# Global attention in arrays of its own, one layer's weight halves on chip, and new begin times, in an adaLN block with windowed attention

## The reference

```python
mod = (silu(c) @ wmod).reshape(8, 6, 1, 256)          # sa, ca, ga, sb, cb, gb
h = layernorm(x) * (1 + ca) + sa
x = x + ga * global_attention(h)                      # causal over 1024 rows, RoPE, one softmax per row
h = layernorm(x) * (1 + cb) + sb
x = x + gb * ffn(h)                                   # DEPTH = 2 local layers
# a local layer:
h = shift_token(x); q, k, v = split(h @ wqkv)         # 256 -> 3 x 512, 8 heads of 64
q, k = rotary_xpos(l2norm(q) * qs, l2norm(k) * ks)
x = x + local_attention(q, k, v) @ wo                 # windows of 128, each looks one window back
h = layernorm(shift_token(x)) * lg + lb
a, g = split(h @ w1 + b1); x = x + (a * gelu(g)) @ w2 + b2
```

## Time and profile before

| | |
|---|---|
| median of 3 runs | 2667.91 us (2666.67 to 2672.59) |
| the profiled execution's own time | 2665.09 us |
| its span, first to last instruction | 2663.3 us |
| TensorE matmul busy | 2533.0 us, 95% |
| VectorE, ScalarE, GpSimd busy | 85%, 73%, 49% |
| mean granted TensorE clock | 0.985 of full |
| DMA, mean over the span | 17 GB/s |

### The profile page before, as it was taken

The page is one execution under the profiler, slowest core; times in us unless marked ns, Lnnn a source line. Parts: engine busy times, 40 slices in busy tenths (PEclk is TensorE's granted clock), DMA queues, the critical chain, the costliest instruction groups (busy, mean ns, idle before and its releaser), DMA issues. The chain is left out here.

```text
span 2663.3 us, 71937 instructions
## 1 busy us (share of the span) xinstructions
PE 2533.0 (95%) x25566; PEld 1726.5 (65%) x25566; DVE 2274.1 (85%) x6823; ACT 1932.2 (73%) x4782; POOL 1300.6 (49%) x953
## 2 busy tenths in 40 slices
PE   7899989999899998999989999999999999989997
PEld 4566666667566665676656666666766666666675
DVE  8897889878898788987889878898889978799785
ACT  3598856878468784778747787587874888648884
POOL 2364534655355553555435554365544555445552
PEclk7999999999999999999999999999999999999999
DMA  5000010000100000000000000000000000000000
GB/s 190 21 7 8 5 43 2 9 6 8 39 3 9 6 16 30 4 10 4 18 29 5 9 5 20 25 6 8 6 19 25 6 8 6 19 25 6 7 6 21
DMA packets 51026, 46.49 MB, mean 17 GB/s; under 512 B 11530, under 2 KB 47980, under 8 KB 50548
## 3 DMA queue, kind: packets, MB, share of 16 engines
q1 hardware_dynamic: 50004, 40.78, 5.0%
q10 hardware_dynamic: 672, 1.10, 0.1%
HBM read 25.06 MB, written 8.42 MB: 13 GB/s over the span
## 5 line engine op out<-in xcount | busy, mean ns | idle before, releaser
L780 ACT ACTIVATE ar_b<-ar_b,small 128x192 f32<-128x192 f32 (+1 forms) x1024 | 445.3, 437 | 80.7 <-DVE small L1073 79.8
L1343 POOL TENSOR_TENSOR ar_c<-ar_c 128x1024 f32<-128x1024 f32 x128 | 302.7, 2365 | 284.0 <-DVE ar_c L1059 283.2
L1339 POOL TENSOR_TENSOR small<-small,neg_half 128x16 f32<-128x16 f32 x128 | 380.6, 2974 | 115.0 <-DVE small L1031 112.0
L1073 DVE CUSTOM_DVE_ANT_0 ar_b<-ps,mask_t,small 128x192 f32<-128x192 f32 x896 | 318.9, 411 | 27.0 <-PE ps L529 26.8
L1358 POOL TENSOR_TENSOR mlp<-mlp 128x512 f16<-128x512 f32 x160 | 198.0, 1243 | 204.2 <-ACT mlp L835 203.6
L160 PE MATMUL ps<-wqkv_hi,ht_hi 128*128 128x512 f16 x768 | 292.9, 381 | 0.0
L162 PE MATMUL ps<-wqkv_hi,ht_lo 128*128 128x512 f16 x768 | 291.6, 380 | 0.0
L161 PE MATMUL ps<-wqkv_lo,ht_hi 128*128 128x512 f16 x768 | 291.6, 380 | 0.0
L160 PE MATMUL ps<-ht_hi,w_hi 128*128 128x512 f16 (+1 forms) x704 | 269.1, 382 | 11.3 <-DVE ht_lo L1021 11.3
L162 PE MATMUL ps<-ht_hi,w_lo 128*128 128x512 f16 (+1 forms) x704 | 268.3, 381 | 0.0
L161 PE MATMUL ps<-ht_lo,w_hi 128*128 128x512 f16 (+1 forms) x704 | 268.1, 381 | 0.0
(11 more groups left out here) (197 smaller groups left out, 6911.7 us busy)
## 6 DMA issues: line engine op xcount, KB each, us to landing
xu<-in_L_attn_x_dram SPq DMA_DIRECT2D x32, 256.0 KB, 2.9
out_dram<-xu SPq DMA_DIRECT2D x64, 128.0 KB, 2.5
rows<-xu SPq DMA_DIRECT2D x128, 63.5 KB
mlp<-in_L_ffn_wqkv_dram SPq DMA_DIRECT2D x2, 1536.0 KB, 6.6
modb<-mod_rows SPq DMA_DIRECT2D x8, 384.0 KB, 4.3
rows<-in_L_ffn_w_dram SPq DMA_DIRECT2D x2, 1364.0 KB, 10.3
rows<-xu SPq DMA_DIRECT2D x112, 0.5 KB
ar_b<-in_L_wmod_dram SPq DMA_DIRECT2D x2, 768.0 KB, 7.1
```

The lines of the kernel that those rows point to most:

```text
L780: last = act.activation(pw, pw, ACT.Exp, bias=mnw[:, n % 2, h:h + 1], scale=-1.0, accum_out=smw[:, n % 2, h:h + 1])
L1073: last = dve.tensor_tensor_reduce(out=PW[:, pw_at(f, q, i) + c:pw_at(f, q, i) + KW], in0=ps[:, bk, i * KW + c:(i + 1) * KW], in1=mask, sca ...
L1339: pool.tensor_tensor(rinv[:, n % 4, :], ssm[:, n % 2, :], neg_half[:, 0:16], ALU.pow).then_inc(s_rinv, 1)
L1343: pool.tensor_tensor(M1[:, n % 2, :], M1[:, n % 2, :], M2, ALU.add).then_inc(s_add, 1)
```

## The change

- Global attention gets arrays of its own: a new `ar_g` (`xn1`, `hf1`, `ra`, `rb`, `P1`, `PT1` and new halves of h, `hg`), and the windows' `V`, `QT`, `KT` go into a new `ar_w`. Its waits for the last window of the batch before are gone. To fit, `xn1`, `hf1`, `rb`, `P1`, `PT1` hold one tile in place of two, and the windows' `V` three in place of four; so `rw`, `af`, `rp`, `pe` and `ph` now wait for the reader of the tile just before.
- The input rows are loaded into an array of their own, `XI`, almost a batch ahead.
- Only one layer's weight halves and xpos table stay on chip. The halves of both layers are stored in DRAM in the first batch (`tq`, `tw`, `tv`, `to`, `tx`), and each of the 15 further layers reloads its own: `lq` 1.5 MB, `lw` 1.4 MB, `lv` 0.79 MB, `lo` 0.52 MB, `lx` 1 MB, all issued by the sync engine on its one queue, in a place set by the table.
- `PERIOD` goes from 316.98 to 313.02, and all begin times are new.

```diff
-        wqkv_p = [sb(f"wqkv_{s}", [P, DEPTH, NC, 3 * INNER], F16) for s in ("hi", "lo")]
+        wq_r = sb("wqkv", [P, 2 * NC * 3 * INNER], F16)
+        wqkv_p = wq_r[:, :].rearrange("p (s c n) -> p s c n", s=2, c=NC)
...
+        XI = sb("x_in", [P, NT, DIM])
-        V = ar_a[:, 0:2048].rearrange("p (r n) -> p r n", r=4)
+        ar_w = sb("ar_w", [P, 16 * 256])
+        V = ar_w[:, 0:1536].rearrange("p (r n) -> p r n", r=3)
...
-        xn1 = ar_c[:, 0:1024].rearrange("p (r t c n) -> p r t c n", r=2, t=2, c=NC)
+        ar_g = sb("ar_g", [P, 20 * 256])
+        xn1 = ar_g[:, 0:512].rearrange("p (t c n) -> p t c n", t=2, c=NC)
+        P1 = ar_g[:, 2560:3584]
+        PT1 = [ar_g[:, 3584 + 512 * i:4096 + 512 * i].bitcast(F16).rearrange("p (k n) -> p k n", k=NT) for i in range(2)]
+        hg = [ar_g[:, 4608 + 256 * i:4864 + 256 * i].bitcast(F16).rearrange("p (c n) -> p c n", c=NC) for i in range(2)]
...
                         if b:
-                            sp.wait_ge(s_fin, (b - 1) * NT + 2 * p + 2)
-                        sp.dma_start(X[:, 2 * p:2 * p + 2, :],
+                            sp.wait_ge(s_x2, at("ys", b - 1, 2 * p + 1))
+                        sp.dma_start(XI[:, 2 * p:2 * p + 2, :],
...
+                    elif k == "lq":
+                        L = piece[1]
+                        if L:
+                            for q in range(3):
+                                sp.wait_ge(s_qkv, at("E", L * NT - 1, q))
+                            if L == 1:
+                                sp.wait_ge(l_t, 64 * DEPTH)
+                            sp.dma_start(wq_r[:, :], halves[0][L % DEPTH]).then_inc(s_lq, 16)
+                    elif k == "lx":
+                        L = piece[1]
+                        if L:
+                            sp.wait_ge(s_m, at("x1", L * NT - 1))
+                            if L == 1:
+                                sp.wait_ge(l_tx, 16 * DEPTH)
+                            sp.dma_start(xp_r[:, :], halves[4][L % DEPTH]).then_inc(s_lx, 16)
...
                         act.wait_ge(s_hf, at("af", b, p))
-                        if b:
-                            act.wait_ge(s_w1g, at("Wg", DEPTH * b - 1, p // 2, NJ))
-                            act.wait_ge(s_w1, at("Wa", DEPTH * b - 1, p // 2, NJ - 1))
-                        act.activation(ht[0][:, :, 1 + p * 256:1 + (p + 1) * 256], hf1[:, p % 2], ACT.Copy).then_inc(s_hh, 1)
+                        if p:
+                            act.wait_ge(s_proj, at("pj", b, 2 * p - 1))
+                        elif b:
+                            act.wait_ge(s_proj, at("pj", b - 1, NT - 1))
+                        act.activation(hg[0], hf1, ACT.Copy).then_inc(s_hh, 1)
...
-                        if i >= 2:
-                            act.wait_ge(s_ptr, at("pt", b, i - 2, (i - 2) // 4))
+                        if i:
+                            act.wait_ge(s_ptr, at("pt", b, i - 1, (i - 1) // 4))
                         elif b:
-                            for f in range(2):
-                                act.wait_ge(s_ht, at("H", last_n(b), f))
+                            act.wait_ge(s_ptr, at("pt", b - 1, NT - 1, 1))
...
-PERIOD = 316.98
+PERIOD = 313.02
-    ("N", "pe"): {(0, 0): 123.5, (0, 1): 132.94, (0, 2): 175.55, (0, 3): 188.69, (1, 0): 261.37, (1, 1): 261.81,
-        (1, 2): 307.93, (1, 3): 314.11},
+    ("N", "pe"): {(0, 0): 118.73, (0, 1): 130.84, (0, 2): 183.67, (0, 3): 189.19, (1, 0): 256.91, (1, 1): 260.05,
+        (1, 2): 308.74, (1, 3): 312.67},
-        9: 289.33, 10: 305.28, 11: 308.37, 12: 335.38, 13: 337.27, 14: 339.78, 15: 341.64},
+        9: 287.57, 10: 304.28, 11: 310.15, 12: 335.46, 13: 338.78, 14: 348.91, 15: 352.88},
-    ("qt", "pe"): {0: 3.02, 1: 4.76, 2: 26.52, 3: 33.18, 4: 39.83, 5: 48.07, 6: 52.14, 7: 54.22},
+    ("qt", "pe"): {0: 8.13, 1: 9.86, 2: 20.92, 3: 25.32, 4: 34.03, 5: 45.42, 6: 49.01, 7: 51.45},
-    ("sc", "pe"): {0: 6.49, 1: 8.61, 2: 29.63, 3: 36.02, 4: 43.41, 5: 50.14, 6: 54.68, 7: 57.67},
+    ("sc", "pe"): {0: 11.59, 1: 12.42, 2: 24.29, 3: 31.02, 4: 38.18, 5: 49.44, 6: 51.89, 7: 54.87},
```

More of the change, by code:

```diff
@@ L166, in adaln_kernel @@
         s_x = [sem(f"x_loaded{p}") for p in range(NT // 2)]
-        s_xs = [sem(f"shifted_rows{p}") for p in range(DEPTH * NT // 2)]
+        s_xs = [sem(f"shifted_rows{p}") for p in range(NT // 2)]
         s_out = [sem(f"out_stored{w}") for w in range(NT)]
@@ L470, in _ @@
                         for kb in range(i + 1):
-                            last = mm3(pe, ps[:, bk, 0:DIM], [q[:, i % 2, kb, :] for q in PT1],
+                            last = mm3(pe, ps[:, bk, 0:DIM], [q[:, kb, :] for q in PT1],
                                        [q[:, kb, :] for q in V1], kb == 0, kb == i)
@@ L588, in _ @@
                         for c in range(NC):
-                            last = mm3(pe, ps[0:m, bk, :], [q[:, L % DEPTH, c, 2 * j + i, 0:m] for q in w1_p],
+                            last = mm3(pe, ps[0:m, bk, :], [w1_p[:, q, c, 2 * j + i, 0:m] for q in range(2)],
                                        [q[:, c, a:a + 512] for q in ht], c == 0, c == 1)
@@ L606, in _ @@
                                 mm3(pe, ps[:, bk, 0:DIM], [q[j][:, a:a + P] for q in (uh, ul)],
-                                    [q[:, l, j, :] for q in w2_p], j == 0, False)
+                                    [w2_p[:, q, j, :] for q in range(2)], j == 0, False)
                             else:
                                 for s in range(2):
-                                    last = pe.matmul(ps[:, bk, 0:DIM], u_tail[:, a:a + P], w2_p[s][:, l, NJ, :],
+                                    last = pe.matmul(ps[:, bk, 0:DIM], u_tail[:, a:a + P], w2_p[:, s, NJ, :],
                                                      start=False, stop=(s == 1))
@@ new lines @@
+    ("zR", "pe"): {(): -27.46},
+    ("zT", "pe"): {(): -29.95},
+    ("zW", "pe"): {(): -20.82},
+    ("za", "act"): {(): -32.69},
+    ("zb", "sp"): {(): -3},
+    ("zc", "sp"): {(): -32.22},
+    ("zd", "act"): {(): -25.07},
+    ("ze", "act"): {(): -29.06},
+    ("zf", "dve"): {(0,): 19.92, (1,): 79.05},
+    ("zg", "sp"): {(): -24.38},
+    ("zh", "act"): {(): -23.49},
+    ("zi", "dve"): {(): -26.78},
+    ("zk", "dve"): {(): -24.55},
+    ("zl", "dve"): {(): -22.62},
+    ("zm", "sp"): {(): -10.54},
```

388 lines of the change are left out of this document (231 added, 157 removed), and 731 rows, old and new, of tables (BEGIN, EDGE).

## The result

The changed kernel took 2684.51 us (median of 4 runs, 2682.93 to 2686.37) against 2667.93 us before: a ratio of 1.0061, 95% interval 1.0045 to 1.0077. It is slower by 16.6 us, where 26 less were forecast.

A forecast was written before the change was run, and what follows sets the result against it. TensorE was taken as the bound, busy 2533.0 of 2663.3 us, so only its 130 us idle could be won. Terms -36 + 8 - 4 + 4 + 1 + 0.7 = -26 gave 2642 us, range 2628 to 2661.

The forecast's parts named there:

- Its base on the plan: Gaps between TensorE pieces taken from the new begin-time table, large ones scaled by 0.9; no durations taken from it.
- Global attention freed: Where global attention ran almost alone, window pieces fill TensorE's idle 6.1 us down to 1, in seven places: -36 us.
- The new wait before `N`: Layer end: `N` (1, 2) waits 2.6 us for `ls` on VectorE, other waits shrink; net +1.0 in eight batches, +8.
- The reloads: 5.3 MB for each of 15 layers on the sync queue, covered by 30 us: counted 0, bound +19 us.
- The rival had the right queue: Shifts wait behind the reloads: window 13's shift stands behind `lx`; 2661 us at +19, 2652 at half; 8%.
- The first batch: Loads in another order and some 10 MB stored to DRAM before `ls`: +4 us, bounds 0 and +10.
- The clock: Clock falls about 40 us after the first transposes cost 8 us in six periods; half won back: -4, bounds 0 and -8.
- the third rival: Clock falls at the new wait before `N`, 6.8 us at half clock per batch: 2673 us, 2658 with half the batches; 6%.
- Single arrays: `pe`, `ph` waits for the tile before covered: 0, bound +45; as slower rival, 0.70 in each of 64 tiles, 2687; 8%.
- loads don't slow the engines: VectorE's L922 took 524 ns under up to 321 GB/s of loads and 535 later, so no price.
- The tail: The last batch's chain of 33.8 us, its pieces as before: +0.7 us for a later `Y`.
- no gain: Period bound by VectorE's and ScalarE's order, the waits only move: about 2666 us; 7%.

The follow-up runs named there:

- The cut of GpSimd's work: Both kernels with rope sum for 32 of 1024 columns, k scaling for one head of eight, lo half set to 0: changed 2652.97 us, before 2666.09.
- The one moved piece: `x1` of window 1 put back behind the last two modulations in the changed kernel: 2672.91 us; put ahead of them in the kernel before: 2696.71.
- early stores: Changed kernel with seven of the ten first-batch stores at other places of the sync queue, six where it is idle, one behind the second shift: 2674.33 us.
- late reloads: On top of early stores, reloads of w2 (second layer) and wo, wqkv behind it, wait until VectorE has read the shifted rows: 2667.13 us.
- the last run: The best version with the layer norm of the second layer's third pair moved ahead of the next batch's statistics and a residual on VectorE: 2657.52 us.
- the best version: Changed kernel with early stores, late reloads, `x1` of window 1 later and `nm` of window 5 earlier: 2645.88 us, ratio 0.9919 to the kernel before.

## Why the prediction was wrong

**Its base on the plan, the step that failed.** The prediction said that "the plan's large gaps come out at 0.9 of their size; small ones are swallowed", and took gaps and no durations from the new table. The large ones did so again: 2.6 planned before `N` (1, 2) and 2.46 measured, 1.50 before `J` 15 and 1.42 measured. But gaps of nothing came out at 2.03 before `D` (0, 3), 1.2 before `av` (1) and 0.6 at `H`, because durations on VectorE are no property of the instruction: they depend on what GpSimd executes beside it, and the new table changed that. The cut of GpSimd's work gives the size of this: 31.5 us in the changed kernel, about half of it through the clock, against 1 in the one before. The one moved piece shows the mechanism in both directions, and order alone wins back 21 of the 31.5: from 2667.13 us with early stores and late reloads to 2645.88 when `x1` of window 1 and `nm` of window 5 are moved too.

**Global attention freed, -36.** The waits of the earlier trace rows for `ql` (2.52) and `hl` (1.20) are gone, but the term was mis-sized at both ends. The same stretch of the fourth batch, in the kernel before and in the changed one:

```profile
1348.80:1382.80 34.00, 29.71 (x181) 19.44 (x179) 28.75 (x88) 12.64 (x24) 13.62 (x15) 0.85 0.14 47
```

```profile
1349.50:1383.50 34.00, 31.56 (x200) 19.38 (x199) 30.75 (x92) 22.15 (x39) 17.36 (x17) 1.00 0.17 55
```

The 6.1 of the earlier trace rows came from the only one of six batches in which the clock stayed at 1.00 here; the others idled 4.3 to 5.1, with a granted clock of 0.85 to 0.95, and the mean of the six is 4.9. After the change the six idle 2.3 to 3.2 and not 1, 2.5 on average, with the clock at 1.00 in all of them; the 3.2 of the result holds a wait of 1.50 before `pj` 1 that only the third batch has. So the idle time falls by 2.4 in each of seven batches, -17 us. Part of what is left is the same thing as above: a residual beside GpSimd's work (L1091) takes 1.32 us, where its median is 0.42, and `av` (1) waits behind it.

```profile
1043.58 1.32 DVE L1091 TENSOR_TENSOR xu<-xu,x_in 128x256 f32<-128x256 f32 x1
...
1046.20 0.28 PE L179 MATMUL ps<-ar_a,ar_g 128*128 128x256 f16 x1 [1.18 <-DVE ar_g L1075]
```

**The new wait before `N`, +8.** It came as described, 2.46 us, the longest of the period. The waits before `pj` 0 and `Wg` are gone, and one of up to 0.4 stands before `pj` 1 now. So more was regained than the 1.3 of the sum: the waits of the place come to 4.2 to 4.7 us a batch (5.7 in the third), where those of the earlier trace rows came to 4.8, and the net is about nothing and not +1.0. That it would be set by VectorE's order was only half right, as the last run showed: the shift behind `J` 15 bounds the place.

**The reloads, 0.** They cost 8.9 us. The rival had the right queue and the wrong side: not the shift behind a reload is late, but the one just ahead of it, by some 0.4 to 0.6 us, at the ends of layers where VectorE waits for it. The shift behind `lx` did take 3.79 us to issue, but its reader came later still, as the sum had it. Late reloads regain 7.2 of the 8.9; what the other 1.7 are stays open.

**The first batch, +4 with +10 as the bound.** The stores cost 12.1 us, and 10.2 of it go when they are only placed elsewhere. Here shifts did stand behind 6 MB on the queue, with 5.71 us for a shift that is otherwise issued in 1. The sum had seen this and priced it with a rate at which it almost fitted.

**The clock, -4.** It did not come: the mean clock is 0.986 after 0.985. The falls some 40 us behind the first transposes, in five of seven batches before, are gone, as the term had it. But a fall now comes in each of seven batches behind the wait before `N`, as the third rival had it, of 3.4 us, half of what it priced, and in two batches another behind the wait before `D` (0, 3). In the best version the mean is 0.988. One such fall in the windows of the changed kernel, half clock (1.2 GHz):

```profile
1345.40:1348.80 3.40, 3.40 (x17) 2.32 (x16) 2.68 (x11) 0.00 (x0) 0.94 (x2) 0.50 0.71 295
```

**Single arrays, 0; loads don't slow the engines.** Both hold: no wait for the tile before stands among TensorE's longer waits, and VectorE's busy time is the same with and without reloads.

**The tail, +0.7.** It is 32.5 us, 1.3 shorter.

The misses that an experiment sized, 31.5 - 1 for the held instructions, 8.9 for the reloads and 12.1 - 4 for the stores, are 47.5 us, against 42.6 between forecast and result. That they come so near is partly luck. The sum leaves out global attention (+19) and `N` (-8), and these overlap with the 31.5, which holds the wait before `av` (1) and some 15 us of clock. The rival "no gain: the period is bound by VectorE's and ScalarE's order, and the waits only move" came nearest in its mechanism. By number the single arrays came nearest, with 2687 us, but that would have been luck: they cost nothing. The rival "no gain" got 7%, because TensorE idled only 1.4 of 234 us in the dense part before; that spoke of the old order alone.

## What to carry to other kernels

A plan whose durations are constants can't be trusted in its small gaps when VectorE and GpSimd work at the same time: look which instructions will lie side by side in the new order before pricing a gap at nothing. A DMA that is hidden by tens of microseconds of cover can still cost, through the small urgent transfers ahead of it and behind it on its queue; put bulk where no urgent one is in flight. And when a large change moves the time little, compare the busy time of each engine first: 48 us more on VectorE with the same instructions named the cause before any experiment.

## What the runs showed of the hardware

VectorE's instructions with their duration (min/median/max in ns) over the changed kernel. Two read only SBUF, two read PSUM, one is a reduction:

```profile
L1114 DVE SCALAR_TENSOR_TENSOR xu<-xu,stats,modb x64: 483/485/2380, 60.4 to 2403.3; 128x256 f32<-128x256 f32 x64
L1134 DVE TENSOR_SCALAR small<-small x128: 174/175/1306, 92.7 to 2604.5; 128x16 f32<-128x16 f32 x128
L1212 DVE TENSOR_TENSOR xu<-ps,xu x128: 406/418/426, 137.8 to 2639.2; 128x256 f32<-128x256 f32 x128
L1251 DVE SCALAR_TENSOR_TENSOR mlp<-ps,bias,mlp x192: 732/751/758, 192.8 to 2668.6; 128x512 f32<-128x512 f32 x160, 42x512 f32<-42x512 f32 x32
L1129 DVE TENSOR_REDUCE small<-ar_c x128: 1165/1211/1222, 91.5 to 2603.3; 128x16 f32<-128x1024 f32 x128
```

The first two can take five and seven times as long; the two that read one operand from PSUM, and the reduction, never vary by more than 5%, though GpSimd works beside them as well. It looks like a stop and not a slowdown: even the scaling of 16 columns takes up to 1.3 us, and the stretched L1114 ends 0.3 us behind GpSimd's add. The Trainium skill says this ("SBUF — State Buffer", section "Who interferes with whom"): a VectorE instruction with two SBUF inputs contends with a GpSimd instruction that reads SBUF, one with at most one SBUF input, outside the modes with two ports, does not, nor does a reduction, and the blocked engine waits for the whole instruction of the other. The trace agrees in each of these rows, and the short `tensor_scalar` is among the forms that this page of the Trainium skill lists as able to enter a mode with two ports. In one thing the trace is narrower than the rule: GpSimd's `pow` over 16 columns (L1442, 2.90 us) reads SBUF too, and L1114 beside it took its 0.49 us. This page of the Trainium skill also says that DMA does not contend with the engines; VectorE's 2321.8 us without reloads, against 2322.4 with them, agree.
